# The expert-key stage of a two-layer attention and expert kernel, with the third and fourth heads' logits moved up beside the down products

## What is computed

```python
q = einsum('btd,ed->bte', h, W_q)             # h: normed x
sim = einsum('pbthn,hkpn->pbthk', q, keys)    # 4 heads, 2 halves, 64 keys
sx, sy = top_k(sim, 8)
scores = top_k(sx[..., :, None] + sy[..., None, :], 8)
w = silu(einsum('btd,bthkd->bthk', h, down_embed[indices]) * softmax(scores))
experts = einsum('bthk,bthkd->btd', w, up_embed[indices])
dense = silu(h @ W_up.T) @ W_down.T
```

## Time and profile before

| | |
|---|---|
| runs of the kernel | 1182.7, 1174.91, 1180.41 us, median 1180.41 |
| span of the profiled execution | 1177.9 us |
| its own time | not given beside the span; the runs' median is 2.5 us above the span |
| expert-key stage | 312.9 us (`hidden(0)`) to about 680 us |
| a pair of steps, 9 and 10 | 496.48 to 540.93: 44.45 us |

### The profile page before, as it was taken

The page is one execution under the profiler, slowest core; times in us unless marked ns, Lnnn a source line. Parts: engine busy times, 40 slices in busy tenths (PEclk is TensorE's granted clock), DMA queues, the critical chain, the costliest instruction groups (busy, mean ns, idle before and its releaser), DMA issues.

```text
span 1177.9 us, 17014 instructions
## 1 busy us (share of the span) xinstructions
PE 1048.4 (89%) x5486; PEld 651.9 (55%) x5486; DVE 796.8 (68%) x1989; ACT 644.2 (55%) x858; POOL 497.0 (42%) x550
## 2 busy tenths in 40 slices
PE   8889999989878989889899699999999888899991
PEld 3444444434457778778777563334334333688881
DVE  7766786886888787787785146777777946344443
ACT  3356655655656766766765613565555560355550
POOL 6558786785415334335344411114123336122220
PEclk9799999999999999999999895998998998899996
DMA  7844967645999000000003401365364318222226
GB/s 238 256 134 153 285 225 279 185 154 194 276 256 258 20 1 1 1 1 1 0 28 82 117 9 54 113 192 144 91 172 108 106 50 349 62 69 73 74 62 214
DMA packets 74201, 149.88 MB, mean 127 GB/s; under 512 B 7823, under 2 KB 44577, under 8 KB 72580
## 3 DMA queue, kind: packets, MB, share of 16 engines
q1 hardware_dynamic: 61380, 98.80, 30.9%
q0 software_dynamic: 10800, 47.63, 11.2%
q10 hardware_dynamic: 1936, 2.36, 0.6%
HBM read 73.14 MB, written 76.25 MB: 127 GB/s over the span
## 4 chain that ended last, share of the span: by engine, by line
PE 58%; DVE 24%; ACT 8%; issue 5%; DMA 2%; POOL 2%; SPq 1%; another core or an unknown queue 0%; DVEq 0%; ACTq 0%; POOLq 0%
PE ps L1270 14%; PE ps L1400 9%; DVE negmax L1811 7%; PE ps L1367 7%; PE ps L1381 5%; PE ps L1343 4%; PE ps L1352 3%; PE ps L1614 3%; PE ps L1591 2%; PE ps L1577 2%; PE ps L1409 2%; PE ps L1735 2%; DVE hl L1816 1%; DVE moe_w L2156 1%; POOL w_first L866 1%
## 5 line engine op out<-in xcount | busy, mean ns | idle before, releaser
L1811 DVE TENSOR_REDUCE negmax<-ps 128x1 f32<-128x512 f32 x512 | 322.2, 683 | 64.9 <-PE ps L1367 64.2
L1061 ACT ACTIVATE pt<-ps 128x1024 f32<-128x1024 f32 x256 | 257.8, 1027 | 163.3 <-PE ps L1381 161.2
L1367 PE MATMUL ps<-sk,sq 56*128 56x512 f32 (+1 forms) x512 | 157.5, 451 | 31.2 <-DVE negmax L1811 19.1
L1400 PE MATMUL ps<-pt,v_aug 128*32 128x512 f32 x1024 | 148.6, 649 | 0.9 <-POOL pt L762 0.7
L1381 PE MATMUL ps<-sq,sk 57*128 57x512 f32 (+1 forms) x512 | 133.7, 504 | 2.3 <-DMA sq<-m_sb 1.6
L762 POOL TENSOR_TENSOR pt<-pt,near 128x256 f32<-128x256 f32 x128 | 92.3, 731 | 69.4 <-ACT pt L1061 68.9
L1367 PEld LDWEIGHTS ps<-sk,sq 56*128 56x128 f32 (+1 forms) x512 | 72.7, 201 | 83.5 <-DVE negmax L1811 60.2
L1381 PEld LDWEIGHTS ps<-sq,sk 57*128 57x128 f32 (+1 forms) x512 | 52.2, 194 | 105.1 <-issue 73.9
L954 POOL DMA_INDIRECT expert_out<-yo,dest x39 | 38.1, 977 | 117.0 <-ACT yo L1236 102.4
L866 POOL TENSOR_TENSOR w_first<-w_first,moe_w 128x1024 f32<-128x1024 f32 x16 | 38.1, 2380 | 105.1 <-DVE pt L2148 104.4
L1577 PE MATMUL ps<-sel,hl 128*128 128x512 f32 x256 | 72.9, 418 | 5.1 <-DVE pt L2148 5.1
(11 more groups left out here) (323 smaller groups left out, 2042.1 us busy)
## 6 DMA issues: line engine op xcount, KB each, us to landing
expert_rows<-zero SPq DMA_DIRECT2D x3, 5586.0 KB, 53.6
expert_weights_split<-wst POOLq DMA_DIRECT2D x8, 2048.0 KB, 8.9
qk_rows<-hl SPq DMA_DIRECT2D x30, 512.0 KB, 2.8
sk<-qk_rows SPq DMA_DIRECT2D x62, 192.0 KB, 4.9
sq<-qk_rows SPq DMA_DIRECT2D x62, 192.0 KB, 4.5
moe_w<-in_w POOLq DMA_DIRECT2D x16, 512.0 KB, 7.1
wexp<-expert_weights_split POOLq DMA_DIRECT2D x16, 512.0 KB, 4.8
wexp<-expert_weights_split SPq DMA_DIRECT2D x4, 2048.0 KB, 13.9
```

The source lines that it names most:

```text
L1061: act.activation(pt[:, 4 * (U % 2) + 2 * half:4 * (U % 2) + 2 * half + 2, :], ps[:, 2 + 2 * half:4 + 2 * half, :], ACT.Exp, scale=(BIAS, S ...
L1367: pe.matmul(ps[:, job.bank, :], sq[r, pair, t * P:(t + 1) * P], sk[r, pair, :], start=True, stop=True).then_inc(s_job, 1)
L1400: ins = pe.matmul(ps[32 * j:32 * j + 32, OBANK, :], v_aug[:, b % 2, c, HG * g + j, :], pt[:, 4 * (U % 2) + j, :], start=(c == 0), stop=(c ...
L1811: dve.tensor_reduce(negmax[:, n % 2, col:col + 1], src, AX, ALU.max, negate=True).then_inc(s_jd, 1)
```

## The change

On PE `logits(s, 2)` moves up between the two halves of the down products, and `logits(s, 3)` right behind the second half, both ahead of the first `add_experts`. On ACT `weights_copy` is split in its two halves, with `expand(s, 2)` between them, and `expand(s, 3)` follows `small_exp`, ahead of `sim_copy`. No instruction is added or left out. DVE, POOL and SP keep their order.

```diff
             for s in range(NTL):
...
                 if s >= 3:
-                    weights_copy(s - 3)
+                    weights_half(s - 3, 0)
+                if s:
+                    expand(s, 2)
+                if s >= 3:
+                    weights_half(s - 3, 1)
                 if s:
                     small_exp(s)
-                    expand(s, 2)
+                    expand(s, 3)
                 if s + 2 < NTL:
                     sim_copy(s + 2)
                 if s == 15:
                     first_values(0)
-                if s:
-                    expand(s, 3)
...
                 if y >= 0:
                     turn_weights(y, 0)
                     ff_down(y, 0)
+                if s:
+                    logits(s, 2)
+                if y >= 0:
                     turn_weights(y, 1)
                     ff_down(y, 1)
+                if s:
+                    logits(s, 3)
+                if y >= 0:
                     add_experts(y, range(0, 3))
                 if s == 15:
                     first_values(0)
-                if s:
-                    logits(s, 2)
...
                 if y >= 0:
                     add_experts(y, range(3, 6))
-                if s:
-                    logits(s, 3)
```

More of the change, by code:

```diff
@@ L1149, in _, with weights_half @@
             act.copy(ff1s[0], wff1[:]).then_inc(s_wh, 1)
+            def weights_half(n, i):
+                if n:
+                    act.wait_ge(s_yu, n)
+                front_copy(accT[:, 512 * i:512 * i + 512], ("at", n, i))
             def weights_copy(n):
                 for i in range(2):
-                    if n:
-                        act.wait_ge(s_yu, n)
-                    front_copy(accT[:, 512 * i:512 * i + 512], ("at", n, i))
+                    weights_half(n, i)
             def row_high(kind, i):
```

## The result

The changed kernel took 1194.92 us, median of 4 runs (1189.06 to 1197.78), beside 1177.71 (1174.91 to 1182.7) for the kernel before: a ratio of 1.0113 [1.0064, 1.0161], slower by 1.1%, outside the predicted range of 1171.5 to 1191. Run twice more, it took 1191.48 and 1190.82, ratios 1.0122 [1.0053, 1.019] and 1.0076 [1.005, 1.0102]. The profiled execution took 1193.19 us with a span of 1191.3.

What follows compares the result with a forecast made beforehand. DVE and what it waits for were taken to bound odd steps, PE even ones. Step changes of -8.2 us plus 9.4 us of low clock gave +1.2 us, a median of 1181.6 us, range 1171.5 to 1191.

Steps and rivals of the forecast that it cites:

- What bounds the kernel, and the waits: Odd steps set by DVE, even by PE; the odd step's end pause becomes a 3.6 us middle one.
- The sum without the clock: All step gains and losses of the stage with the clock staying up: -8.2 us.
- the forecast's 23.15: Length in us of a changed odd step at full clock, 0.15 us longer than before.
- the five pairs: Odd and even steps 3 to 12: 43.5 us a pair against 44.45, -4.75 us in all.
- steps 1 and 2: Step 1 gains 0.65 us, step 2 gains 0.
- step 13: PE's new middle pause costs in full there, so step 14 starts 1.5 us later.
- from step 15 to the attention: Step 15 gains 4.7 us from early exponentials and shorter PE waits, kept to the stage's end.
- Step 1's gain: 0.65 us, since the exponential that the fourth head's mask waited for can come earlier.
- paid 1.56 a pair: Old order's loss in us: low clock slows even steps' `hidden` after the odd step's end pause, in five pairs.
- The clock's price: Low clock behind the new middle pause: 1.56 us in each of six odd steps (3 to 13), 9.4 in all.
- The slower rival: Clock falls twice as long behind the new pauses: 3.1 us a step, +10.4, 1190.8 us; chance 0.15.
- The row that gave the price its lower end: Profile row at 361.20: a 3.3 us pause left the clock at 1.00, so a price of 0.
- The sum: -8.2 us of steps plus 9.4 of clock: +1.2 us, median 1181.6 us.

Runs made afterwards that it cites:

- form with three products: Changed kernel plus three products of a matrix of ones filling PE's middle pause in odd steps 3 to 13: 1179.08 us, ratio 0.9989.
- experiment 2: Spare products of ones filled PE's pause in odd steps: changed kernel with three 1179.08 us, kernel before with two 1171.7 us.
- experiment 1: Both kernels run again without edit for second profiles: kernel before 1181.8 us, ratio 1.0008; changed kernel 1191.48 us, ratio 1.0122.
- the products ahead of the attention: Two products of ones (1.7 us) put ahead of the second attention's first score products; in the changed kernel 1186.10 us on chip 11.
- step 15 alone: Kernel before with the new order of logits and exponentials in step 15 only: 1176.62 us, ratio 0.9955.
- both behind: Changed kernel with third and fourth heads' logits both behind the second half of the down products: 1163.56 us, ratio 0.9865; again 1172.34, 0.9899.
- the even steps alone: New order in even steps and step 15, old order in odd steps 1 to 13: 1172.65 us, ratio 0.9942.

## Why the prediction was wrong

**What bounds the kernel, and the waits: right.** The pause moved from the end of the odd step to its middle (3.80 us, 3.6 forecast), is gone ahead of even steps' `hidden`, and is 1.35 us (1.25) in the even step. Step 10 took 20.53 (20.35). Only the place of the low stretch was off: it begins with the third logits.

**The sum without the clock: near, with luck in it.** What an odd step takes in the new order at full clock no profile of after shows, and the forecast's 23.15 is not measured. The form with three products does show it, and its third logits start as far into step 9 as in after (10.80 and 10.79 us): 23.4 to 23.5, and 24.6 in step 13. By these the odd steps 5 to 11 of after took 2.8, 1.6, 1.3 and 2.6 us more for the clock and step 13 took 1.6 more. Rows of after's steps 5, 7 and 13, then step 13 with the products:
```profile
407.33:433.60 26.27, 22.46 (x109) 18.95 (x108) 20.04 (x52) 15.05 (x19) 8.88 (x7) 0.87 0.01 2
453.85:478.90 25.05, 21.24 (x110) 18.10 (x108) 19.75 (x52) 15.06 (x19) 8.47 (x5) 0.93 0.00 1
590.69:616.92 26.23, 22.49 (x110) 18.48 (x107) 19.64 (x53) 15.15 (x19) 10.80 (x17) 0.93 0.07 26
...
579.36:603.98 24.62, 23.71 (x116) 18.28 (x113) 19.68 (x53) 15.15 (x19) 10.87 (x17) 1.00 0.07 26
```
With that taken out, the profile gives -4.0 us for the five pairs (forecast -4.75), +0.4 for steps 1 and 2 (-0.65), +1.7 for step 13 (+1.5), +0.4 for step 14 (+0.4) and -4.5 from step 15 to the attention (-4.7): -6.0 against -8.2. Step 1's gain did not come. Of the -4.5, step 15 up to its up products gave 3.3, in every profile of after; the other 1.2 lie behind it, where the 18 profiles take 60.4 to 63.1 us whatever the order of their logits, and the first profile of before took the most. That is luck. And the five pairs measured the new order at full clock against an old one that paid 1.56 a pair. Held against each other at full clock (experiment 2), the steps themselves lose about 1 us a pair; and before doesn't always pay (experiment 1).

**The clock's price: right in kind and in the sum, the latter by luck.** The stretches cost 9.9 us in all over five steps, where I had 9.4 over six. Step 3 had a low stretch too, which cost it nothing but 0.25 us of the step. The slower rival, a stretch twice as long, is what steps 5 and 11 did (steps 7 and 11 in the second profile); the others cost 1.3 to 1.6, near the 1.56 that I took from one row. Why some steps have two low stretches in a row is open. The row that gave the price its lower end was no rule either: behind the same pause at the end of step 2 `hidden` ran at full speed in before and at the lower clock in after.
```profile
364.51 2.97 PE L1270 MATMUL ps<-sk,hl 128*128 128x512 f32 x12 [3.27 <-DVE wff L2156]
```
```profile
365.55 4.58 PE L1275 MATMUL ps<-sk,hl 128*128 128x512 f32 x12 [3.23 <-DVE wff L2163]
```
The Trainium skill (TensorE: Matmul & The Clock Gate, the section on terms) prices low time at half; of about 24 us at the lower level in these five steps that makes an estimate of 12, more than the 9.9 measured.
So the stage came to -6.0 + 9.9 = +3.9, as measured between the first two profiles, forecast +1.2.

**The step that failed: "The sum".** It took everything behind the stage as unchanged, a term put at nothing without a reason. The second attention, which has the same instructions, took 8.7 us more. Over all 18 profiles of this case its length follows its time at the lower level, 245.4 us + 0.28 per us low (27 to 75 us low, 252.0 to 266.7 us long; correlation 0.98). The forecast of +1.2, the 2.7 us by which the stage missed it, this 8.7 and the 0.8 outside both make the +13.4 of the profile. The trace of before would have shown the exposure, a mean clock of 0.92 there over 258 us, had I asked for that window. The runs say that this is no accident of one profile: the attention took 266.5, 263.0 and 265.8 us in the three profiles of the plain changed kernel and 257.8 and 259.1 in the two of before, and the plain changed kernel had a mean clock of 0.922 to 0.931 in each of its 16 runs, the same kernel with the products ahead of the attention 0.931 to 0.945 in 20.

How the loss divides is less sure than this pair of profiles makes it look. The medians put after 17.2, 11.4 and 8.7 us above before in three groups. The attention has 4 to 9 us of that by the profiles, and the stage 4 to 10, since before's own stage took 398.2 us in its second profile. So the stage was underpriced too: the forecast let the old order pay its 1.56 in all five pairs, as one profile showed it.

The Trainium skill says in the same page, under "What's actually happening", that the observation runs free of the kernel's start. The runs agree in part: the same program's low stretches differ in place and length from execution to execution (experiment 1, and 252.0 against 263.8 for one kernel). But the changed kernel had 65 to 75 us of low clock in its second attention in all three of its plain profiles, and before 40 and 48 in its two, so the free running doesn't make it even from kernel to kernel. What fixes it was not tried, and stays open.

**Chances.** 0.09 on slower by over 1% was too low: it priced only the doubled low stretch, and no mechanism outside the stage.

**The best version.** Both heads' logits behind the second down half, with the two products ahead of the attention: 1162.5 us, ratio 0.9811 [0.976, 0.9862] against before on the same chip, and 0.9865 or 0.9899 without the products. Its stage, 386.6 us, is the part that doesn't hang on the attention's clock.

## What to carry to other kernels

A wait moved from a step's end to its middle is still a wait: count what its idle time does to TensorE's clock, and compare both orders at the same clock (fill the pause with spare products) before crediting an order with what the clock gave. An order that breaks one long pause into several short ones can gain where moving it loses. And a change in one stage can move the clock in a later one with the same instructions, so a forecast for a kernel whose mean clock is below 1 needs a term, of either sign, for stages that the change does not touch. One profile of the kernel before is not enough for such a sum: low stretches that it shows can be missing in the next.

## What was not expected of the hardware

- Less than 2 us of products ahead of an attention of 260 us took 7 to 10 us off the median. Two profiles on one chip differ by 14 us there (265.8 and 252.0), with 67 us at 1.2 GHz in the one and 27 in the other; another profile with the products has 263.8.
- The kernel's time follows its mean granted clock from run to run: over 98 runs of the kernel before (1171.2 to 1193.3 us, clock 0.949 to 0.924) a fitted line gives 8.0 us for 0.01 of clock, and the runs scatter 2 us about it. Brought to 0.940 by this line, before stands at 1178.7, after at 1181, step 15 alone at 1175.4, both behind and the even steps alone at 1169 to 1170. That ranks the orders as their stages do, but takes out the part of an order's cost that goes through the clock: after stands 2 us above before there, where the medians have 9 to 17.
- Chips or sessions differ by as much as the change did: before had medians of 1176.96, 1180.07, 1182.1 and 1186.22 us in four groups.
